# A selective scan with expert layers on one core: C repeated over partitions by DMA, du*B whole in PSUM, the state over it, an fp32 first layer, remainders of B on GpSimd, loops unrolled

## The reference

```python
xn = layernorm(x)
# branch 1: selective scan, 16 states per channel
deltaBC = xn @ W_deltaBC.T                  # 64 + 16 + 16 columns
delta   = softplus(deltaBC[:64] @ W_dt.T + b_dt)
deltaA  = exp(delta * A);  BX = delta * B[n] * xn
h[t]    = deltaA[t] * h[t-1] + BX[t]        # for each channel and n
y       = sum_n h * C[n] + D * xn
# branch 2: 8 experts, each takes the 128 tokens of a batch with its highest probability
G, I = top_k(softmax(xn @ Wg.T), 128)
out[I] += G * (gelu(xn[I] @ W1[e] + b1[e]) @ W2[e] + b2[e])
```

## Time and profile before

| | us |
|---|---|
| median of 3 runs | 2723.78 (2721.72 to 2727.97) |
| the profiled execution, its own time | 2724.12 |
| its span | 2722.1 |
| busy TensorE, VectorE, ScalarE, GpSimd | 2370.1, 2605.7, 2012.5, 2226.7 |
| first du*B of the main stage starts | 208.49 |
| last product on VectorE starts | 2685.08 |
| mean granted clock of TensorE | 0.974 of full speed |

### The profile page before, as it was taken

How to read it: one execution, slowest core, us unless ns; L and a number is a source line. 1 busy time by engine, 2 the same in 40 slices (tenths; PEclk the granted TensorE clock), 3 DMA queues, 4 the chain that set the end, 5 groups by cost and what they waited for, 6 DMA issues and landing times. The chain is left out here.

```text
span 2722.1 us, 42941 instructions
## 1 busy us (share of the span) xinstructions
PE 2370.1 (87%) x13036; PEld 1837.6 (68%) x13036; DVE 2605.7 (96%) x2829; ACT 2012.5 (74%) x3437; POOL 2226.7 (82%) x1290
## 2 busy tenths in 40 slices
PE   6738898989998999899998899899999998999985
PEld 2316776777777777777777777777777777777774
DVE  5699999999999999999999999999999999999994
ACT  6636777777777777777777777787777777777772
POOL 4415888988888988988888988888888898888885
PEclk9858999999999999999999999999999999999998
DMA  9971232232223232232323222222323223222222
GB/s 337 354 279 31 77 95 75 53 66 52 52 54 67 54 65 47 54 66 35 71 52 67 54 57 54 51 51 56 68 52 70 43 51 68 49 55 54 35 37 33
DMA packets 123272, 206.87 MB, mean 76 GB/s; under 512 B 14112, under 2 KB 98176, under 8 KB 122752
## 3 DMA queue, kind: packets, MB, share of 16 engines
q0 software_dynamic: 70656, 100.70, 21.2%
q1 hardware_dynamic: 50992, 102.79, 11.1%
q10 hardware_dynamic: 1360, 0.26, 0.1%
HBM read 117.70 MB, written 100.66 MB: 80 GB/s over the span
## 5 line engine op out<-in xcount | busy, mean ns | idle before, releaser
L467 POOL TENSOR_TENSOR ysum<-ysum,prod 128x1024 f32<-128x1024 f32 x480 | 1311.9, 2733 | 69.4 <-DVE prod L946 67.1
L937 DVE TENSOR_TENSOR_SCAN state<-decay,bank_x 128x1024 f32<-128x1024 f32 x512 | 1165.6, 2277 | 10.2 <-issue 8.3
L1157 PE MATMUL bank_l<-w_sb,hid 128*128 128x256 f32 x4096 | 994.8, 385 | 0.0
L1157 PEld LDWEIGHTS bank_l<-w_sb,hid 128*128 128x128 f32 x4096 | 757.3, 190 | 148.3 <-issue 10.2
L1139 PE MATMUL bank_l<-ext_hi,w_hi 128*128 128x256 f32 x2048 | 653.0, 319 | 2.2 <-ACT og L676 0.4
L872 DVE TENSOR_TENSOR bank_x<-du,bank_b 128x512 f32<-128x512 f32 x1024 | 648.1, 677 | 2.4 <-PE bank_b L1048 2.1
L614 ACT ACTIVATE decay<-delta,a_sb 128x511 f32<-128x511 f32 x1024 | 640.0, 707 | 12.7 <-POOL delta L432 11.9
L624 ACT ACTIVATE hid<-bank_l,b_st 128x256 f32<-128x256 f32 x1024 | 421.5, 472 | 279.1 <-PE bank_l L1139 277.4
L946 DVE TENSOR_TENSOR prod<-state,bank_c 128x1024 f32<-128x1024 f32 x512 | 619.7, 1210 | 8.2 <-PE bank_c L1099 8.1
L1139 PE MATMUL bank_l<-ext_lo,w_hi 128*128 128x256 f32 x2048 | 583.3, 285 | 0.0
L1139 PE MATMUL bank_l<-ext_hi,w_lo 128*128 128x256 f32 x2048 | 580.8, 284 | 0.0
(11 more groups left out here) (115 smaller groups left out, 2107.1 us busy)
## 6 DMA issues: line engine op xcount, KB each, us to landing
decay<-in_x SPq DMA_DIRECT2D x32, 512.0 KB, 6.7
xn_rows<-decay POOLq DMA_DIRECT2D x32, 512.0 KB, 6.3
xn_cols<-delta SPq DMA_DIRECT2D x32, 512.0 KB, 5.7
w_raw<-in_w SPq DMA_DIRECT2D x32, 512.0 KB
w_sb<-in_w SPq DMA_DIRECT2D x16, 1024.0 KB, 6.2
xnt<-xn_cols SPq DMA_DIRECT2D x32, 512.0 KB, 3.7
out<-yrow POOLq DMA_DIRECT2D x32, 512.0 KB, 6.1
ex<-xn_rows,idx_st POOLq DMA_INDIRECT x256, 2.8
```

The costliest lines, as they stand in the source:

```text
L467: nc.gpsimd.tensor_tensor(ysum[:, m % 2], first, prod[:, i], ALU.add).then_inc(sum_done, 1)
L937: nc.vector.tensor_tensor_scan(state[:, i % 2].rearrange("p c t -> p (c t)"), decay[:, k % 2, i].rearrange("p c t -> p (c t)"), bank_x[:, ...
L1157: i = nc.tensor.matmul(o, hid[:, (k - 1) % 2, f, c * K:(c + 1) * K], w2_sb[:, le2, f], start=False, stop=(f == FC - 1))
```

## The change

- **C by DMA.** `take_bc` copies all 96 columns of deltaBC in fp32 to `bc_all`; SP writes the 16 rows of C to DRAM (`c_rows`) and, for each unit, loads four of them repeated over 128 partitions into `c_all` (1 MB, two buffers). The spread of C by TensorE and `bank_c` are gone. `load_c(u+1)` is issued when unit u - 1 has made its last product.
- **du*B and state.** `bank_x` has four banks, two pairs used in turn. du*B is one instruction of 1024 columns, and the scan writes the state over it in the same banks. The product reads the state from PSUM and C from SBUF. It holds the banks until the next du*B but one.
- **First layer in fp32.** W1 is loaded whole (`w1_sb`, two buffers, 1 MB each) and used as it is: one fp32 matmul in place of three fp32r ones; `round_w1`, `split_w1` and `ext_low` are gone. `expand` is one fp32 matmul from `bc_all`, and `take_low` is gone.
- **Remainders of B on GpSimd.** `take_rest` and `take_lo` work on 96 partitions from SBUF, `take_rest` behind the sum of step 0 of slot 1, `take_lo` behind the sum of step 3 of slot 1. A third small transfer moves the lo part into `bcs`, for which SP waits in slot 1's `move_parts`.
- **Unrolled.** The main stage has no hardware loop; all indices are constants, and the copies to fixed places are gone. A scatter waits only for the scatter two units before from the same buffer (and for y of its batch where that came first); y waits only for the last scatter to its own batch.

```diff
             def move_parts(nb, par, used):
+                held(all_done, nb)
+                sp.dma_start(c_rows[nb - 1], bc_all[BC - N:BC, :]).then_inc(c_out, 16)
...
+                held(lo_done, nb)
+                sp.dma_start(bcs[64:96, par], bc_lo[64:96, :]).then_inc(lo_moved, 16)
+            def load_c(u):
+                held(c_out, (u // SLOTS + 1) * 16)
+                held(prod_done, (u - 1) * STEPS)
+                first = u % SLOTS * STEPS
+                sp.dma_start(c_all[:, u % 2], c_rows[u // SLOTS:u // SLOTS + 1, first:first + STEPS, :]
+                             .broadcast_to([P, STEPS, T])).then_inc(c_in[u % 2], 16)
...
# GpSimd
+            def take_rest(nb):
+                pool.wait_ge(all_done, nb)
+                pool.wait_ge(hi_done, nb)
+                wait(pool, lo_done, nb - 1)
+                nc.gpsimd.tensor_tensor(bc_rest[0:BC, :], bc_all[:], bc_hi[0:BC, :], ALU.subtract).then_inc(rest_done, 1)
+            def take_lo(nb):
+                pool.wait_ge(mid_done, nb)
+                wait(pool, lo_moved, nb * 16 - 16)
+                nc.gpsimd.tensor_tensor(bc_lo[0:BC, :], bc_rest[0:BC, :], bc_mid[0:BC, :], ALU.subtract).then_inc(lo_done, 1)
...
+                            wait(pool, scattered[w % 2][c], w // 2 * 16)
...
# ScalarE
             def take_bc(nb):
                 act.wait_ge(bc_proj, nb)
+                wait(act, rest_done, nb - 1)
+                wait(act, z_done, nb * 2 - 2)
+                wait(act, c_out, nb * 16 - 16)
+                nc.scalar.copy(bc_all[:], bank_t[0:BC, :]).then_inc(all_done, 1)
                 wait(act, hi_moved, nb * 16 - 16)
-                nc.scalar.copy(bc_hi[64:96, :], bank_t[64:96, :]).then_inc(hi_done, 1)
+                nc.scalar.copy(bc_hi[0:BC, :], bank_t[0:BC, :]).then_inc(hi_done, 1)
...
# VectorE
-                lone = odd
-                for dt in (lone, 1 - lone):
...
-                    nc.vector.tensor_tensor(bank_x[:, at:at + T], du[:, par, dt], bank_b[:], ALU.mult).then_inc(bx_done, 1)
+                wait(dve, prod_done, s - 1)
+                nc.vector.tensor_tensor(bank_x[:, s % 2].rearrange("p (c t) -> p c t", c=HC), du[:, par],
+                                        bank_b[:][:, None, :].broadcast_to([P, HC, T]), ALU.mult).then_inc(bx_done, 1)
...
+                        nc.vector.tensor_tensor_scan(bank_x[:, s % 2], decay[:, k % 2, i].rearrange("p c t -> p (c t)"),
+                                                     bank_x[:, s % 2], 0.0, ALU.mult, ALU.add).then_inc(scan_done, 1)
...
+                        if i == 0:
+                            dve.wait_ge(c_in[u % 2], (u // 2 + 1) * 16)
...
+                        nc.vector.tensor_tensor(prod[:, i], bank_x[:, s % 2].rearrange("p (c t) -> p c t", c=HC),
+                                                c_all[:, u % 2, i][:, None, :].broadcast_to([P, HC, T]),
+                                                ALU.mult).then_inc(prod_done, 1)
...
# TensorE
-                            if q % 2 == 1:
-                                wait(pe, prod_done, s)
-                                nc.tensor.matmul(bank_c[:], pick[:, N + n:N + n + 1].broadcast_to([3 * 2 * N, P]),
-                                                 bcs[:, m % 2], start=True, stop=True).then_inc(c_ready, 1)
...
-                                    for w, m_ in ((w1_hi, ext_hi), (w1_hi, ext_lo), (w1_lo, ext_hi)):
...
+                                    i = nc.tensor.matmul(bank_l[(q + k) % 2][:, (f % 2) * UT:(f % 2 + 1) * UT],
+                                                         w1_sb[:, e2, hc, f * P:(f + 1) * P], ext[:, k % 2, hc],
+                                                         start=(hc == 0), stop=(hc == HC - 1))
```

More of the change, by code:

```diff
@@ L51 @@
 LATE = 6
-W1_PARTS = 4
 EPS = 1e-5
@@ L84, in build @@
         xn_rows = nc.dram_tensor("xn_rows", [NB * T, D], F32, kind="Internal").ap()
+        c_rows = nc.dram_tensor("c_rows", [NB, N, T], F32, kind="Internal").ap()
         xn_cols = nc.dram_tensor("xn_cols", [NB, P, HC, T], F32, kind="Internal").ap()
@@ L344, in main @@
             def main(j):
-                for m in range(BODY):
-                    b = j * BODY + m
+                for k in range(BU):
+                    m, sl = k // SLOTS, k % SLOTS
+                    u, b = j * BU + k, j * BODY + m
                     if not there(b, NB):
+                        continue
+                    if there(u + 1, NU):
+                        load_c(u + 1)
+                    if sl == 1 and there(b + 1, NB):
+                        move_parts(b + 2, (m + 1) % 2, b * N)
+                    if sl != 0:
                         continue
@@ L398, in rows @@
                     b = q * ROWS + r
-                    if isinstance(q, int) and b == NB:
-                        for piece in range(W1_PARTS // HC):
-                            split_w1(0, 0, 0, piece)
                     if there(b, NB):
@@ L438, in take_du @@
                 nc.gpsimd.tensor_tensor(du[:, par], delta[:, par], xnt[:, par], ALU.mult).then_inc(du_done, 1)
-            for piece in range(W1_PARTS // HC):
-                split_w1(0, 0, 1, piece)
+            take_rest(1)
+            take_lo(1)
             pool.wait_ge(picks_done, 2)
-            stage_idx(0, 0)
-            gather(0, 0, 0, 1, 0)
-            gather(1, 1, 0, 1, 0)
+            gather(0)
+            gather(1)
+            y_before = {}
             def main(j):
@@ L469, in main @@
                             take_delta(b + 2, (m + 1) % 2)
-                            wait(pool, bx_done, b * N * HC)
+                            wait(pool, bx_done, b * N)
                             take_du(b + 2, (m + 1) % 2, (j * 2 + (m + 1) // 2 + 1) * 16)
-                        if i % 2 == 1 and sl == 2 and there(u, NU - BU // 2):
-                            split_w1(j * 2 + k // 8 + 1, (k // 8 + 1) % 2, m % 2, i // 2)
+                        if sl == 1 and i == 0 and there(b, NB) and there(b + 1, NB):
+                            take_rest(b + 2)
@@ L474, in main @@
+                        if sl == 1 and i == 3 and there(b, NB) and there(b + 1, NB):
+                            take_lo(b + 2)
                         if i == 0:
-                            if sl == 2 and there(b + 1, NB):
-                                wait(pool, scattered, u * 32 - 64 * 2)
-                                stage_idx((m + 1) % BODY, b * 8 + 8)
                             if there(u + 2, NU):
-                                nm = ((k + 2) // SLOTS) % BODY
-                                gather(k, (sl + 2) % SLOTS, nm, b + (2 if sl >= 2 else 1), u + 1)
+                                gather(u + 2)
@@ new lines, in main @@
+                            pool.wait_ge(yrow_done, y * 2 + 2)
+                            wait(pool, y_added, 16 * y)
+                            last = [w for w in range(min(u - 1, NU)) for c in range(UB) if batch_of(w, c) == y]
+                            if last:
+                                pool.wait_ge(scattered[last[-1] % 2][y % UB], (last[-1] // 2 + 1) * 16)
+                            y_before[y] = True
+                            pool.dma_start(out_tiles[y], yrow[:], accum_op=ALU.add).then_inc(y_added, 16)
@@ L507, in _ @@
+            through(main, NJ)
         @block.scalar
@@ L512, in _ @@
                 act.dma_start(dst, src).then_inc(params_in, 16)
-            for half in range(2):
-                act.dma_start(b1_all[:, half], b1).then_inc(b1_in, 16)
-            def round_w1(ge, par, hc, used):
-                act.wait_ge(w1_in, (ge * HC + hc) * 16 + 16)
-                wait(act, up_done, used)
-                nc.scalar.copy(w1_hi[:, par, hc], w1_raw[:]).then_inc(w1_hi_done, 1)
+            act.dma_start(b1_all[:], b1).then_inc(b1_in, 16)
             def rows(q):
@@ L689, in main @@
                             take_mid(b + 2)
-                        if pair == 1 and sl == 0 and there(u, NU - BU // 2):
-                            round_w1(j * 2 + e2 + 1, (e2 + 1) % 2, m % 2, (u - k % 8) * 4)
                         if pair == 2 and there(u + 1, NU):
@@ L898, in _ @@
             nc.vector.memset(decay[:, :, :, :, 0:1], 0.0).then_inc(zero_set, 1)
-            between = {1: lambda: take_rest(1), 2: lambda: take_low(1), 3: lambda: take_lo(1, 0, 0), 9: lambda: take_delta(1, 0),
-                       10: lambda: take_du(1, 0, 16)}
+            between = {9: lambda: take_delta(1, 0), 10: lambda: take_du(1, 0, 16)}
             dve.wait_ge(work_in, 2)
```

254 lines of the change are left out of this document (82 added, 172 removed).

## The result

The kernel after takes **2600.37 us** (median of 4 runs, 2596.33 to 2602.73), beside 2723.64 us before (4 runs, 2721.72 to 2727.97): ratio 0.9544, 95% interval 0.9526 to 0.9562. The forecast was 2616 us (2525 to 2685). The profiled execution took 2598.42 us around a span of 2596.7.

What follows compares the result with a forecast made beforehand. The bound was to move from VectorE to TensorE, with waits for ScalarE's GELUs in slot 3. Lead 206 + 32 x 74.4 + tail 27 = 2613.8 us span, 2616 us as time, range 2525 to 2685.

Steps and rivals of the forecast that it cites:

- VectorE's list: VectorE's instructions in the main part: 4.46 us a step and 71.4 us a batch after the change, from 77.4.
- no change: VectorE's scan, writing PSUM instead of SBUF, keeps its time; bounds 0.06 us less and 1.07 us more.
- rival 3: VectorE's scan slows by writing the bank it reads: 1.07 us bound, 88.5 us per batch, 3067 us; chance 0.05.
- TensorE's work: TensorE per batch: spreads of C 3.5 us less, fp32 first layer 6.6 more; 72.4 us, above VectorE's 71.4.
- the base of 69.98: TensorE's profiled busy time in four steady units of 76.69 us, including some 1.4 us of pipeline ends ahead of waits.
- The waits on ScalarE: TensorE idles 1.9 us per batch for GELUs in slot 3 (15.1 us chain), plus 0.1 for take_rest in slot 1.
- The batch: Main part, 16 steps: TensorE's 72.4 us plus waits, 74.4 us in all, times 32.
- The lead: Stretch before the main part: 2.5 us less as splits leave VectorE's top-8 rounds, 206 us from 208.5.
- Covered, by 3 us: GpSimd's load with take_rest and take_lo added needs some 70.9 us per batch, so it does not set the pace.
- Covered by 9 us: C's 1 MB load for slot 3, the worst, lands 12 to 13 us into slot 2, needed at 22.
- Rival 1: VectorE stays the bound at 71.4 us per batch: 2520, with the usual stalls 2535 us; chance 0.20.
- Rival 2: Chains add up through GpSimd's lag at take_rest, unabsorbed waits or late C: batches 76 to 77.2, 2667 to 2705; chance 0.17.

Runs made afterwards that it cites:

- the early table: One-element GELU ahead of each unit's GELU pairs, added to the kernel after with skip term, ln and first row copy moved later in slot 3: 2575.35 us.
- the final experiment: Kernel after plus skip term, ln and row copy later, one-element GELU early, first W1 load later, take_rest on VectorE from PSUM: 2525.53 us, ratio 0.9270 to before.

## Why the prediction was right, and where it was off

The direction, the new bound and its mechanism were right; the sum was 17.1 us high against the profiled span (2613.8 forecast, 2596.7). Term by term:

- **VectorE's list.** Forecast 4.46 a step and 71.4 a batch; measured 4.44 and 71.0. The scan took 2285 ns against 2277 before, so "no change" held between the bounds of 0.06 less and 1.07 more; rival 3 (a turn of its own for every write into the bank being read) is out. The formula of the Trainium skill ("VectorE: DVE Perf Modes", section on the TRN2 errata) would, by an estimate from it, have made the merged du*B worth 0.158 us a step; all three instructions together gave 4.51 - 4.44 = 0.07, so the trace decides for the overlap.
- **TensorE's work.** Forecast 72.4, measured 70.2. I priced every first-layer block at 1.84, between 1.93 and 1.72 (half way is 1.825). The sixteen of a batch now take 1.72 to 1.90 start to start, without the waits, and 1.78 in the mean; those of slot 2 are two from 1503.95 to 1507.50, one from 1508.21 to 1510.04 and one from 1510.47 to 1512.20. That is 1.0 us of the 2.2. The rest is in the base of 69.98, whose busy time holds the ends of matmuls stretched by waits: I took off half of 1.4; with all of it the sum had been 71.7. What is left, 0.5, no run separates.
- **The waits on ScalarE.** Forecast 1.9 + 0.1, measured 3.3. The place (slot 3, chain of 15 us) was right and the size there near (1.63, or 2.4 with og's 0.74); the 0.32 in each of the other slots was missing. It comes from the GELU table load, which does not begin before the GELU's own wait is over (1.15 us ahead of the load at 1542.28); the early table took it away. The 0.1 for take_rest had no wait to match it in after, where TensorE's slot 1 has none ahead of the down block. Moving 1.9 us of ScalarE's work out of slot 3's chain gave 35 us, which is the confirmation that I trust most.
- **The batch.** 74.4 forecast, 73.54 measured: two errors, 2.2 too much and 1.3 too little, that partly cancel; the closeness of the total is in part luck. 32 batches would give 2353.3; the two long ones add 9.9, and the edges take 3.8, which makes the main part 2359.4 against a forecast of 2380.8. The lead was 3.7 us longer than forecast (W1's first load in the first stage, which I had not costed; without it there the lead is 204.35), the tail 0.5.
- **GpSimd.** Take_rest and take_lo cost 2.85 a batch, forecast 2.6 (1185 and 1661 ns by their groups; the second writes bf16). "Covered, by 3 us" held for its load as a whole, not for take_rest's place in the queue: once TensorE's idle was being taken away, the same chain came back, first with 0.66 us a batch and then with 1.9. The factor in the Trainium skill ("GPSIMD Engine Reference", section "Performance versus the Vector engine") had given an estimate of 2.7, nearer than my 2.6; the trace agrees in the sum within 0.15 us, but not piece by piece (1.19 and 1.66, where the factor gives 1.35 each).
- **C's transfer.** "Covered by 9 us" was true for VectorE and false for the kernel, by 10 us, through the scatter beside it.
- **Rivals.** Rival 1 (VectorE stays bound, 2520 to 2535) did not come true for this kernel, but the final experiment, 2525.5, is what it describes: it needed three moves on other engines. Rival 2's mechanism showed in two batches of 32, in slot 1 of every batch once the skip term was moved, and in full in the kernel with the early table.

## What to carry to other kernels

When a change moves the bound to an engine that runs in order, list what its neighbours do between the two points where they meet: here 1.9 us of work that nobody waited for, on an engine busy 75% of the time, cost 35 us by standing in the wrong place. Cost edits in combination: the early table load lost 10 us until the wait that it uncovered was mended too, and then belonged to a gain of 13 in the main part. And before an elementwise operation goes to the slow engine "because it has room", look at where its operands lie: with one in PSUM it cost VectorE 0.7 us, with both in SBUF beside GpSimd's sum 3.2.

## What was not expected of the hardware

- A VectorE subtraction of 96 x 512 with both inputs in SBUF takes 3.2 us (up to 4.0) beside GpSimd's sum, and 0.68 and 0.75 in the two batches where the sum lay beside it for 0.52 and 0.19 us only; with one input in PSUM it is 0.67 wholly inside the same sum.
- TensorE's granted clock fell to 0.57 behind idles of 1.57 and 2.33 us, and 16 matmul records took 6.47 us in place of 3.72; behind the same idle of 1.9 us it fell in some batches (0.72, 5.41 us) and not in others (1.00, 3.72 us).
- ScalarE's GELU table load starts only when the wait of the activation behind it is over (95.6 us of idle ahead of 128 loads, ended by TensorE); a one-element activation ahead of it brings it forward, for 0.1 us more (0.20, of which half overlaps).
- A scatter that lands in 3.9 us in the median took 8.3 with a 1 MB load issued 0.8 us behind it, and without the loads of C no batch is long.
